# Layer norm by pairs of tiles with GpSimd's applies, no f32 copy of the rows, one copy of both accumulators

## The reference

```python
xn = (x - mean(x)) / sqrt(var(x) + 1e-5)
# attention, 16 heads of 64
Q, K, V = xn @ Wq + bq, xn @ Wk + bk, xn @ Wv + bv
o = softmax(Q @ K.T / 8) @ V                  # per head, over 4096 rows
o = relu(o @ Wo + bo)
a = (o - mean(o)) / sqrt(var(o) + 1e-5)
# experts
e = argmax(xn @ Wr.T)                         # one of 8 for each row
h = gelu(xn @ W1[e] + b1[e])                  # 4096 wide
y = h @ Wo2 + bo2 + xn
f = (y - mean(y)) / sqrt(var(y) + 1e-12) * gamma + beta
out = x + a + f
```

## Time and profile before

| | us |
|---|---|
| median of 3 runs | 1857.01 |
| lowest, highest | 1852.81, 2019.57 |
| profiled execution | 1858.14 |
| its span, slowest core | 1856.6 |
| spans of the other cores | 1843.0 to 1853.4 |
| first exp starts | 147.34 |
| last exp starts | 1245.0 |
| last scatter is started | 1844.89 |

### The profile page before, as it was taken

One profiled execution on the slowest core, in us unless ns is written; L12 is line 12 of the kernel. 1 busy time (PEld: TensorE's weight loads), 2 busy tenths in 40 slices (PEclk: granted clock), 3 DMA queues, 4 the chain that ended last, 5 costly groups with the idle time before them and its releaser, 6 DMA issues.

```text
span 1856.6 us, 43286 instructions; the slowest of 8 cores (1843.0 to 1856.6 us)
## 1 busy us (share of the span) xinstructions
PE 1672.6 (90%) x15784; PEld 945.0 (51%) x15784; DVE 730.6 (39%) x1348; ACT 1352.4 (73%) x1540; POOL 322.5 (17%) x357
## 2 busy tenths in 40 slices
PE   3778998999999999999999997879699999999995
PEld 2554554454554454554554553334466666666652
DVE  4762453452452453443443544228203233323133
ACT  4878998999999999999999999986433332233210
POOL 1110000001000000000000000001222344533335
PEclk8999999999999999999999999999899999999998
DMA  8984445336455435445444446735866766666622
GB/s 203 265 214 75 70 70 85 71 70 98 81 93 86 69 70 92 73 72 86 70 70 69 70 81 148 170 70 192 285 215 199 230 205 215 216 213 205 223 75 95
DMA packets 54207, 244.05 MB, mean 131 GB/s; under 512 B 8176, under 2 KB 8816, under 8 KB 51696
## 3 DMA queue, kind: packets, MB, share of 16 engines
q0 software_dynamic: 25056, 137.91, 36.3%
q1 hardware_dynamic: 28368, 102.84, 17.3%
q10 hardware_dynamic: 576, 0.45, 0.1%
HBM read 295.69 MB, written 105.91 MB: 216 GB/s over the span
## 4 chain that ended last, share of the span: by engine, by line
PE 81%; issue 6%; DVE 5%; ACT 3%; DMA 2%; POOL 1%; another core or an unknown queue 0%; DVEq 0%; ACTq 0%; POOLq 0%; SPq 0%
PE acc L910 24%; PE sc L899 14%; PE zp L700 14%; PE yp L713 11%; PE fb L802 8%; PE fb L807 5%; PE yp L988 3%; PE fb L817 1%; DVE stA L1402 1%; DVE stB L1403 1%; DMA stB<-wr_c 1%; ACT xnT L1112 1%; DMA xg<-xseq,idxg 1%; ACT P L1129 1%; ACT xnb L1095 1%
## 5 line engine op out<-in xcount | busy, mean ns | idle before, releaser
L1129 ACT ACTIVATE P<-sc,negm 128x1024 bf16<-128x1024 f32 x1024 | 1061.9, 1125 | 37.1 <-PE sc L899 31.9
L910 PE MATMUL acc<-P,V 64*128 64x512 bf16 x4096 | 627.1, 377 | 29.8 <-DVE stB L1403 29.2
L899 PE MATMUL sc<-QT,KT 64*128 64x512 bf16 x2048 | 405.2, 379 | 49.4 <-issue 29.5
L700 PE MATMUL zp<-xeT,w1r 128*128 128x288 bf16 x2048 | 294.3, 290 | 15.1 <-ACT hT L1035 15.0
L1035 ACT ACTIVATE hT<-zp,small 128x288 bf16<-128x288 f32 (+2 forms) x256 | 119.9, 470 | 249.3 <-PE zp L700 233.1
L910 PEld LDWEIGHTS acc<-P,V 64*128 64x128 bf16 x4096 | 224.7, 94 | 133.5 <-issue 56.4
L713 PE MATMUL yp<-wo,hT 128*128 128x512 bf16 x1088 | 271.5, 379 | 0.0
L899 PEld LDWEIGHTS sc<-QT,KT 64*128 64x128 bf16 x2048 | 123.2, 93 | 268.5 <-issue 237.3
L700 PEld LDWEIGHTS zp<-xeT,w1r 128*128 128x128 bf16 x2048 | 202.4, 99 | 111.4 <-issue 16.5
L625 POOL DMA_DIRECT2D w1bf<-w_c x128 | 63.0, 493 | 899.2 <-ACT P L1129 899.2
L802 PE MATMUL fb<-xnT,wqkv 64*128 64x512 bf16 x1344 | 215.5, 378 | 3.2 <-DVE KT L1251 0.6
(11 more groups left out here) (149 smaller groups left out, 1192.9 us busy)
## 6 DMA issues: line engine op xcount, KB each, us to landing
w1bf<-w_c POOLq DMA_DIRECT2D x128, 512.0 KB, 5.6
w1r<-w1bf SPq DMA_DIRECT2D x128, 512.0 KB
xt<-xseq SPq DMA_DIRECT2D x32, 512.0 KB, 6.7
xb_scr<-xnf POOLq DMA_DIRECT2D x16, 512.0 KB, 7.5
wo2bf<-wo_c POOLq DMA_DIRECT2D x16, 512.0 KB, 5.7
wo<-wo2bf SPq DMA_DIRECT2D x16, 512.0 KB, 5.7
res_scr<-rt SPq DMA_DIRECT2D x16, 512.0 KB, 3.9
xn_scr<-xnf POOLq DMA_DIRECT2D x16, 256.0 KB, 6.8
```

The lines of the kernel that those rows point to most:

```text
L700: ins = te.matmul(zp[z % 2][:, 0:CAP], w1r[k % 8][:, kc * 256 + (ic % 2) * 128:kc * 256 + (ic % 2 + 1) * 128], xeT[:, kc * XR + lo:kc * XR ...
L899: ins = te.matmul(sc[n % 2][:, h * 512:(h + 1) * 512], KT[g % 2][h * 64:(h + 1) * 64, c * 128:(c + 1) * 128], QT[g % 2][h * 64:(h + 1) * 6 ...
L910: return te.matmul(acc[h][:, :], V[(n // 128) % 2][lo:lo + 64, c * 192 + h * 64:c * 192 + h * 64 + 128], P[n % 6][lo:lo + 64, h * 512:(h + ...
L1129: se.activation(out=P[n % 6][:, :], in_=sc[n % 2][:, :], func=AF.Exp, bias=negm[g % 2][:, :], scale=0.125).then_inc(s_P, 1)
```

## The change

1. **Front.** The loop takes a pair of tiles (own and partner's) a step, in 20 steps. One square root, one reciprocal and one product serve a pair, on arrays of two columns. ScalarE applies the own tile; GpSimd applies the partner's with a `tensor_scalar`. There are six `xt` buffers in place of four. VectorE no longer waits for constants; the small array and the router's weights have semaphores of their own, waited for where they are read. Two projection units stand in a step, from step 7.
2. **Fourth group.** Its V units are last, and TensorE does them behind scores 0 and 1.
3. **No `xb_scr`.** The f32 rows are neither stored nor gathered. In the feed-forward stage VectorE takes the statistics of the gathered x (`ve_x`), and GpSimd makes the normalised rows from `xg` (`gp_norm`). Gathers wait for no scatter; `gp_norm` does.
4. **Accumulators.** Both lie side by side, VectorE copies them with one instruction of 128x1024, and in the turn where a block begins, TensorE does both score tiles and both fills before it waits for the copy.
5. The small arrays become columns of one, `tiny`; this changes names, not work.

```diff
-    for k in range(4):
+    for k in range(3):
         out.append([("Q", k), ("K", k), ("K", 4 + k), ("V", k), ("NQ", k), ("NK", k),
                     ("V", 4 + k), ("NK", 4 + k)])
+    out.append([("Q", 3), ("K", 3), ("K", 7), ("NQ", 3), ("NK", 3), ("NK", 7), ("V", 3), ("V", 7)])
...
-        acc = [ps(pa, f"acc{j}", 512, F32) for j in range(2)]
+        accAB = ps(pa, "accAB", 1024, F32)
+        acc = [accAB[:, 0:512], accAB[:, 512:1024]]
...
         def gp_gather_rows(ge, b):
             if b >= 2:
-                ge.wait_ge(f_sc[b % 2], 16 * (b // 2))
+                ge.wait_ge(f_b2, b - 1)
+                ge.wait_ge(f_xa, b - 1)
...
+        def gp_norm(ge, b):
+            ge.wait_ge(f_rs, b + 1)
+            if b >= 2:
+                ge.wait_ge(f_sc[b % 2], 16 * (b // 2))
+            ge.tensor_scalar(out=xb[b % 2][:, :], in0=xg[b % 2][:, :], scalar1=rsx[b % 2][:, :],
+                             scalar2=nmx[b % 2][:, :], op0=ALU.mult, op1=ALU.add).then_inc(f_nx, 1)
+            ge.wait_ge(f_nx, b + 1)
+            ge.tensor_tensor(out=xb[b % 2][:, :], in0=xb[b % 2][:, :], in1=bo2s[:, :],
+                             op=ALU.add).then_inc(f_b2, 1)
...
             for t in range(16):
                 j = t % 2
-                ge.wait_ge(s_nm, 2 * t + 1)
+                ge.wait_ge(s_nr, t + 1)
+                if t >= 2:
+                    ge.wait_ge(s_tp, t - 1)
+                ge.tensor_scalar(out=xnb[j][:, :], in0=xt[(2 * t + 1) % 6][:, :], scalar1=rsp[j][:, 1:2],
+                                 scalar2=nmp[j][:, 1:2], op0=ALU.mult, op1=ALU.add).then_inc(s_np, 1)
+                ge.wait_ge(s_nm, t + 1)
                 ge.dma_start(out=xn_scr[t * 128:(t + 1) * 128, :], in_=xnf[j][:, :]).then_inc(s_xns[j], 16)
-                ge.dma_start(out=xb_scr[t * 128:(t + 1) * 128, :], in_=xnf[j][:, :]).then_inc(s_xbs[j], 16)
...
             scores(0)
             scores(1)
+            for key in first[3][6:]:
+                project(key)
...
+                fresh = a >= 0 and a % 32 == 0 and a > 0
                 if n + 2 < 1024:
                     te.wait_ge(s_P, n + 1)
                     scores(n + 2)
+                if fresh:
+                    for two, part, phase, u in plan[0]:
+                        step(g + 1, two, part, phase, u)
+                    te.wait_ge(s_P, n + 2)
+                    scores(n + 3)
+                    for two, part, phase, u in plan[1]:
+                        step(g + 1, two, part, phase, u)
+                    te.wait_ge(s_cp, a // 32)
...
+        def ve_x(ve, link, b):
+            j = b % 2
+            ve.wait_ge(f_xg[j], 16 * (b // 2 + 1))
+            ve.bn_stats(out=bnx[:, 0:6], in_=xg[j][:, 0:512])
+            link(ve.bn_stats(out=bnx[:, 6:12], in_=xg[j][:, 512:1024]))
+            link(ve.bn_aggr(out=mvx[:, :], in_=bnx[:, :].rearrange("p (c s) -> p c s", s=6)))
+            link(ve.tensor_scalar(out=mvx[:, 1:2], in0=mvx[:, 1:2], scalar1=EPS1, scalar2=None, op0=ALU.add))
+            if b >= 2:
+                ve.wait_ge(f_b2, b - 1)
+            ve_rsqrt(ve, link, rsx[j], mvx[:, 1:2])
+            ve.scalar_tensor_tensor(out=nmx[j][:, :], in0=mvx[:, 0:1], scalar=-1.0, in1=rsx[j][:, :],
+                                    op0=ALU.mult, op1=ALU.mult).then_inc(f_rs, 1)
...
         def ve_ffn(ve, link):
+            ve_x(ve, link, 0)
             for b in range(NBLK):
                 j = b % 2
                 last = b == NBLK - 1
+                if b + 1 < NBLK:
+                    ve_x(ve, link, b + 1)
                 ve.wait_ge(f_b2, b + 1)
...
-            ve.wait_ge(s_cst, 16 * 4)
...
-                ve.tensor_copy(out=stA[:, :], in_=acc[0][:, :]).then_inc(s_cp, 1)
-                ve.tensor_copy(out=stB[:, :], in_=acc[1][:, :]).then_inc(s_cp, 1)
+                ve.tensor_copy(out=stAB[:, :], in_=accAB[:, :]).then_inc(s_cp, 1)
```

353 lines of the change are left out of this document (189 added, 164 removed).

## The result

The changed kernel took **1845.47 us** (median of 7 runs, 1842.20 at least) beside 1857.01 for the kernel before on the same chip. The ratio is 0.994, with a 95% interval from 0.9928 to 0.9952: 0.6% faster, which the 2% bound calls no change. In some executions of either kernel the cores of a die show a lower granted clock and are longer (two of the seven here, 1881.49 and 1994.0 us); ratios leave such executions out, and medians of times don't. The forecast was 1818 us, in a range from 1799 to 1843. The profiled execution took 1842.2 us, with a span of 1840.6.

A forecast was written before the change was run, and what follows sets the result against it. It took ScalarE and TensorE to bound attention, TensorE feed-forward, and a four-engine chain fed by saturated DMA queues the front. Front -21, accumulators -24 and end +5 gave -40: 1818 us, range 1799 to 1843.

The forecast's parts named there:

- Term 1: Start of the front: VectorE waits only for x, so the first apply comes earlier, -8.7 us.
- Term 2: Front's pace: less VectorE, ScalarE and DMA work a pair, from 6.76 us to 5.3 and 6.2, -12 us in all.
- Rival 1: Front: pace stays at 6.76 us, set by latency from engine to engine; 1826 us, chance 0.20.
- GpSimd's apply: Front: GpSimd's new apply taken at 2.4 us, costing nothing while under about 4.5.
- rival 4: Front: GpSimd's apply becomes the pace; 1858 us at a price of 8 us, 1874 at 9; chance 0.04.
- Term 3: Ahead of attention: V3 and V7 behind the first scores bring the first exp 3.9 us earlier, -4 us.
- Term 4: Attention: scores and fills ahead of the wait for the accumulators' copy save ScalarE's waits, -24 us.
- rival 2: Attention: the accumulators' wait only moves to scores n+4, TensorE itself being the pace; 1834 us, chance 0.13.
- Term 5: End of feed-forward: x statistics ahead of the block's add delay the last three blocks, +5 us.
- The prediction's own signs: Wrong if pace is above 6.6, exps take over 1090 us, or TensorE waits between 1400 and 1800 us.
- the 3.7 kept back: Front: 3.7 us of the gain held back for losses at hand-overs, making -24.7 into -21.

The follow-up runs named there:

- e11_wait_weights: Changed kernel with VectorE's wait for the constants and router's weights put back ahead of its first statistics: 1867.61 us, ratio 0.9984.
- e8: Changed kernel with its third part undone (f32 rows stored and gathered again, no x statistics or GpSimd norm in feed-forward): 1841.76 us, ratio 0.9893.
- e2: Changed kernel with VectorE's copies of the projections' results moved behind the pair's four bn_stats in the front: 1836.62 us, ratio 0.9873.
- e12_old_last_group: Changed kernel with the last projection group as before, V3 and V7 ahead of scores 0 and 1: 1865.38 us, ratio 0.9958.
- e4: Changed kernel with its accumulator part undone (two copies, TensorE's old order in that turn): 1850.52 us, ratio 0.9966.
- e6: Changed kernel with scores n+4 between the two halves of the values, not behind the second: 1835.74 us, ratio 0.9868.
- e13: The kernel of e6 with seven P buffers in place of six: 1835.26 us, ratio 0.9839 to the kernel before.
- e17: Changed kernel plus edits of e2 and e6, earlier x gather, norm before sum, seven P buffers, no projection steps at two places a block: 1816.32 us, no ratio.

## Why the prediction was wrong, step by step

- **Term 1** was right: -8.0 us for -8.7, and e11_wait_weights shows that it reaches the end (9.1 of 9.6).
- **Term 2** failed at "I take 6.2 for the eight pairs": they took 6.78, as before, and the seven before them 5.80 for 5.3. DMA did fall out of the bound as worked out (a share of 0.84 for 1.01), and without it there is no gain in pace (6.85 in e8); what it would give in the old loop, alone, wasn't run. The step scaled VectorE's busy time by the old ratio of 1.19 and didn't ask where VectorE's copies had moved: to the head of the step, with the wait for the V unit. Put behind the statistics (e2) they gave 5.95, so 6.2 was within reach, but not in the order that was forecast. Rival 1 (the pace stays) described the eight pairs better, from a wait that neither had named. Why the seven took 5.80 stays open.
- **GpSimd's apply** was right in what it costs (nothing) and too dear in price: 1.19 us for 2.4. TensorE nowhere waits for it in the front. The Trainium skill, GPSIMD Engine Reference (Engine selection), has one-input work near line rate, and the trace agrees: 1.19 beside VectorE's 1.23 for a copy of 128x1024. The 2.4 of rival 4 took that section's factor for two inputs, and the apply has one.
- **Term 3** was right: 3.1 us for 4 (e12_old_last_group). The longer last group that Term 2 put at +2.7 cost 0.8 + 3.1 = 3.9.
- **Term 4** failed at "eight values, 0.9 us, before scores n+4, just in time". They take 1.37 us, as the second half waits for the first and nothing covers that, and ScalarE waited 0.59 there: rival 2, with 30 x (0.75 - 0.59) = 5 us of gain by its waits and 7.4 by e4. The rest was behind bounds in a row: the place of scores n+4 (6 us, e6), then the P buffer (a wait of 0.42 us a turn that e13 removed, and it gained 1.4 us, no more than the scatter), then TensorE's steps (some 10 of 14.8 us, e17). One removed alone shows the next.
- **Term 5** had the mechanism (statistics of x ahead of the add, the gather behind the scatter) and mis-sized it: 12.9 + 2.5 us for 5. It had the two rounds of scatter, gather, statistics and add that stand one behind the other, but put 18.3 us from one add to the next (1818.7 to 1837). In the trace it is 23.5 (1782.05 to 1805.54), against 14 of TensorE. Of the 5.2 more, 4.1 are the statistics, 9.1 us (1796.44 to 1805.5) and not 5, as two of their small instructions stood 4.4 us beside a GpSimd add. What the last scatter to the end took, 2.5 us more, left with the part in e8; its cause wasn't looked for.
- **Not in the forecast**: last exp to last matmul lost 5.3 us. Before, it took 580.1 to 592.1 us by core, now 578.7 to 581.3. Core 1 of the kernel before waited 15.0 us for ScalarE there and now 8.3. e8_undo_ffn, which gathers the f32 rows again, has 582.7 us in the median and 579.4 to 587.8 by core, where the kernels without that gather have 580.1 to 581.9 in the median. So the gather is likely a part of it, and half of the 5.3 stays open.
- **The prediction's own signs** of being wrong didn't show: the pace is under 6.6, the exps under 1090, and TensorE of core 1 has no wait from 1400 to 1800 us. They were set where the pieces were at their old values, and a term could lose half of its size without touching them.

In sum: moved less forecast, piece by piece of the first table, is 0.7 + 8.3 + 2.1 + 13.5 - 5.3 + 7.9 + 2.5 = 29.7. Less the 3.7 kept back, that makes -40 into -14; the medians of the spans moved by -14.9 (1851.0 to 1836.1).

## What to carry to other kernels

When a wait is removed, write down the next three things that the waiting engine needs (its input, its output buffer, the feeder's own load) and price each: here single steps gave 1 to 15 us of exps, and only all together (1096.9 to 1065.2) gave the 24, and more, that the first had been credited with. When an order of work is rewritten, look on the pacing engine at what stands first in a step: a copy that waits for a neighbour belongs behind the work that the neighbour waits for. Before adding a stage in front of a block's add "because the engine has room", follow the last two blocks, where the distance between blocks is the feeder's and not the loop's.

## What the runs showed of the hardware

- **A VectorE instruction with two inputs waits for a GpSimd add, even on one column.** A 128x1 product (1800.17) took 2.02 us and the next 2.38, in place of 0.16 and 0.22, each from about the start to the end of a GpSimd add of 2.33 us; a `TENSOR_SCALAR` beside them kept 0.15. The Trainium skill, SBUF — State Buffer (Who interferes with whom), says that a VectorE instruction with two SBUF inputs excludes a GpSimd one that reads SBUF. The trace agrees, and shows that a single column is enough.
- **TensorE's clock fell after an idle time in the front.** Behind 4.36 us without work, eight transposes took 1.72 us, and 1.07 elsewhere. The granted clock was 1.00 ahead of that idle time and 0.55 in the 2.9 us behind it, so mostly the level of 1.2 GHz in place of 2.4, and 1.00 again from 74 us on. From 60 to 80 us it was 0.91, and 1.00 in e2_stats_first. No run separates the clock's share of e2's gain from the order's. Timeline of the changed kernel, then its windows:

```profile
61.80 1.07 PE L901 MATMUL tp<-constf,xnf 128*128 128x128 f32 x8
...
68.93 1.72 PE L901 MATMUL tp<-constf,xnf 128*128 128x128 f32 x8 [4.36 <-ACT xnf L1145]
```
```profile
60.00:64.50 4.50, 4.36 (x66) 3.60 (x63) 2.73 (x7) 4.20 (x5) 1.77 (x2) 1.00 0.72 138
...
68.90:71.80 2.90, 2.87 (x26) 2.48 (x26) 2.67 (x7) 1.87 (x3) 0.72 (x2) 0.55 0.67 127
...
74.00:80.00 6.00, 5.84 (x60) 3.79 (x58) 5.52 (x11) 2.94 (x4) 1.27 (x2) 1.00 0.88 213
```
